# A two-layer recurrent block on eight cores: ScalarE's norms, the sums of LN1, y before V, and P's transpose put at other places in the order

## The reference

```python
# layer 0
xn = layernorm(x)
z = sigmoid(xn @ Wz.T + bz); h = xn @ Wh.T + bh
s = scan(h_t = (1 - z_t + 1e-8) * h_(t-1) + z_t * h_t)
g = silu((silu(xn @ wg.T / 127) * (xn @ wu.T / 127)) @ wd.T / 127)   # hidden 3072, int weights
x = x + s * g
# layer 1
xn = layernorm(x)
q, k, v = xn @ W_qkv.T
s = softmax(q @ k.T / 32) @ v                                      # one head of 1024, no mask
xr, xk = mix(xn, xn shifted by one token; mu_r), mix(...; mu_k)
g = silu(sigmoid(xr @ W_r) * (relu(xk @ W_k) ** 2 @ W_v))
x = x + s * g
```

## Time and profile before

| | us |
|---|---|
| median of 3 runs | 1410.72 |
| the runs | 1189.59, 1410.72, 1429.85 |
| the profiled execution | 1187.59 |
| its span on the slowest core (core 1) | 1186.4 |
| spans of the eight cores | 1180.2 to 1186.4 |
| PE busy | 1158.8 |
| DVE, ACT, POOL busy | 550.9, 259.5, 131.3 |

### The profile page before, as it was taken

How to read it: one execution, slowest core, us unless ns; L and a number is a source line. 1 busy time by engine, 2 the same in 40 slices (tenths; PEclk the granted TensorE clock), 3 DMA queues, 4 the chain that set the end, 5 groups by cost and what they waited for, 6 DMA issues and landing times.

```text
span 1186.4 us, 15396 instructions; the slowest of 8 cores (1180.2 to 1186.4 us)
## 1 busy us (share of the span) xinstructions
PE 1158.8 (98%) x5500; PEld 533.9 (45%) x5500; DVE 550.9 (46%) x707; ACT 259.5 (22%) x323; POOL 131.3 (11%) x241
## 2 busy tenths in 40 slices
PE   4999999999999999999999999999999999999988
PEld 3444444444444444444444444444444444444434
DVE  4244121456664765135566794011234445555545
ACT  3322211121223111112212733523110110111100
POOL 3121111101111111111011122220000000000000
PEclk9999999999999999999999999999999999999999
DMA  8795954455554684454552579994000105446664
GB/s 198 198 141 88 198 85 74 89 108 115 99 108 69 129 171 74 71 90 98 110 112 52 91 123 155 154 152 109 1 19 19 36 18 124 77 111 120 130 140 153
DMA packets 88074, 124.82 MB, mean 105 GB/s; under 512 B 39744, under 2 KB 44096, under 8 KB 88000
## 3 DMA queue, kind: packets, MB, share of 16 engines
q0 software_dynamic: 31104, 65.03, 34.9%
q1 hardware_dynamic: 56896, 58.81, 19.3%
HBM read 159.47 MB, written 20.97 MB: 152 GB/s over the span
## 4 chain that ended last, share of the span: by engine, by line
PE 96%; DMA 1%; DVE 1%; ACT 1%; issue 0%; POOL 0%; SPq 0%; DVEq 0%; ACTq 0%; POOLq 0%
PE PS L156 95%; PE PS L276 1%; DMA S<-S 1%; DMA S<-xtok 1%; ACT S L265 0%; DVE S L160 0%; DVE S L866 0%; ACT S L286 0%; SPq L127 0%; DVE BN L242 0%; PE PS L297 0%; DVE BN L243 0%; POOL MV L253 0%; POOL S L127 0%; PE PS L834 0%
## 5 line engine op out<-in xcount | busy, mean ns | idle before, releaser
L156 PE MATMUL PS<-S 128*128 128x512 bf16 x5264 | 1140.2, 379 | 6.8 <-DMA S<-S 3.9
L156 PEld LDWEIGHTS PS<-S 128*128 128x128 bf16 x5264 | 514.8, 98 | 622.4 <-issue 13.1
L160 DVE TENSOR_TENSOR S<-S,PS 128x512 bf16<-128x512 bf16 x96 | 66.0, 687 | 190.2 <-PE PS L156 180.8
L361 ACT ACTIVATE S<-PS 128x512 bf16<-128x512 f32 x96 | 57.3, 597 | 249.1 <-PE PS L156 234.0
L806 ACT ACTIVATE S<-PS,CB 128x2048 bf16<-128x2048 f32 x16 | 31.5, 1967 | 225.0 <-DVE CB L804 206.0
L160 DVE TENSOR_TENSOR S<-S 128x512 f32<-128x512 f32 (+2 forms) x60 | 62.9, 1048 | 8.6 <-ACT S L513 2.2
L802 DVE TENSOR_REDUCE CB<-PS 128x1 f32<-128x1024 f32 x32 | 39.2, 1224 | 55.7 <-PE PS L835 33.4
L703 DVE SCALAR_TENSOR_TENSOR S<-S,PS 128x1024 f32<-128x1024 f32 x16 | 19.5, 1221 | 82.1 <-PE PS L156 81.6
L424 ACT ACTIVATE S<-PS 128x512 bf16<-128x512 f32 x32 | 19.1, 597 | 173.2 <-PE PS L156 173.2
L127 POOL DMA_DIRECT2D S<-wg x48 | 27.9, 580 | 262.0 <-PE PS L156 234.0
L744 DVE CAST S<-PS 128x512 bf16<-128x512 f32 x32 | 22.1, 691 | 60.2 <-PE PS L156 60.2
(11 more groups left out here) (73 smaller groups left out, 417.6 us busy)
## 6 DMA issues: line engine op xcount, KB each, us to landing
S<-wg POOLq DMA_DIRECT2D x48, 256.0 KB, 5.1
S<-wu POOLq DMA_DIRECT2D x48, 256.0 KB, 5.8
S<-wd POOLq DMA_DIRECT2D x16, 768.0 KB, 7.8
S<-xtok SPq DMA_DIRECT2D x16, 512.0 KB, 10.1
S<-xt SPq DMA_DIRECT2D x16, 512.0 KB, 15.4
x1s<-S SPq DMA_DIRECT2D x16, 512.0 KB, 3.1
S<-x1s SPq DMA_DIRECT2D x32, 256.0 KB, 4.9
out<-S SPq DMA_DIRECT2D x31, 256.0 KB, 2.8
```

The costliest lines, as they stand in the source:

```text
L156: ins = te.matmul(dst, l, r, start=(i == 0), stop=(i == n - 1))
L160: return DVE.did(ve.tensor_mul(o, a, b))
L361: at = ACT.did(se.activation(sil, ps(bg), AF.Silu, scale=1.0 / 127.0))
```

## The change

In LN0, ACT's norm of the next tile is put ahead of its copy of the tile before, for tiles 1 and 2 and again for tile 6; the copy of tile 2 now stands behind DVE's norm of tile 3; the weight pairs are issued earlier on POOL; the warm matmuls go from 12, 12, 12 and 16 to 10, 10 and 12; transposes 4 and 5 are taken apart, 5 going to behind the second unit. In LN1, `sums` and `stat` become one step, so the list has one step less, and the place that took two steps to use them up takes one. The eight y units of the first quarter go ahead of the first eight V units. `p_transpose(j)` goes to directly behind `scores(j)`, except for the first tile of each quarter, where it stays behind the late units and now stands ahead of `recip`.

```diff
@@ -300,22 +300,30 @@
         ln0_rstd(0)
         POOL.after(xk_tok[1])
         w_pair()
-        for i in range(1, 4):
-            ln0_stats(i)
-            ln0_rstd(i)
-            ln0_norm(i - 1, True)
-            ln0_transpose(i - 1)
-            keep_warm(12)
+        ln0_stats(1)
+        ln0_rstd(1)
+        ln0_norm(0, True)
+        ln0_stats(2)
+        ln0_rstd(2)
         w_pair()
+        ln0_norm(1, True)
+        ln0_transpose(0)
+        keep_warm(10)
+        ln0_stats(3)
+        ln0_rstd(3)
+        w_pair()
+        ln0_norm(2, True)
+        ln0_transpose(1)
+        keep_warm(10)
         ln0_norm(3)
         ln0_stats(4)
         ln0_rstd(4)
         w_pair()
+        ln0_transpose(2)
         ln0_transpose(3, True)
-        keep_warm(16)
+        keep_warm(12)
         ln0_stats(5)
         ln0_rstd(5)
-        w_pair()
         ln0_norm(4, True)
         ln0_stats(6)
         ln0_rstd(6)
@@ -324,12 +332,12 @@
             ln0_norm(5, True)
             ln0_stats(7)
             ln0_rstd(7)
+            ln0_transpose(4)
             ln0_norm(6, True)
-            ln0_transpose(4)
-            ln0_transpose(5)
 
         def span1_b():
             ln0_norm(7)
+            ln0_transpose(5)
             ln0_transpose(6)
 
         early0 = [span1_a, span1_b, lambda: ln0_transpose(7, True), lambda: None]
@@ -525,7 +533,7 @@
                 DVE.after(t, st["rstd"][s], xn_ready)
                 xn1_tok[h, s] = mul(dst, tq, rb)
 
-            steps = [lambda: None, cast, sums, stat]
+            steps = [lambda: None, cast, lambda: (sums(), stat())]
             for s in range(2):
                 for q in range(2):
                     steps.append(lambda q=q, s=s: affine(q, s))
@@ -682,7 +690,7 @@
                 rk_free = ACT.did(se.activation(bf(KACT + o * 1024, 1024), rt, AF.Square))
                 w_done(wpos + o, mm)
                 if h == 0:
-                    step(late1, 2 if o == 7 else 1)
+                    step(late1)
                 else:
                     next(more, None)
             wpos += NC8
@@ -754,10 +762,10 @@
             bank_free[b] = y_tok[e, q]
 
         vq = collections.deque((tt, hf) for tt in range(NT) for hf in range(2))
+        for e in range(NC8):
+            y_unit(e, 0)
         for _ in range(8):
             v_unit(*vq.popleft())
-        for e in range(NC8):
-            y_unit(e, 0)
 
 
         ring = collections.deque([4, 5, 6, 7])
@@ -880,6 +888,8 @@
         for j in range(NT):
             q, i = j // 4, j % 4
             scores(j)
+            if i:
+                p_transpose(j)
             if j:
                 spread(j - 1)
             if q < 3:
@@ -891,8 +901,9 @@
                 late.extend([lambda q=q, d=2 * i: av_unit(q - 1, d), lambda q=q, d=2 * i + 1: av_unit(q - 1, d)])
             while len(late) > 2:
                 late.popleft()()
+            if not i:
+                p_transpose(j)
             recip(j)
-            p_transpose(j)
         while late:
             late.popleft()()
         bank_free[0:4] = s_free * 4
```

## The result

The changed kernel takes 1174.05 us (median of 4 runs, 1173.38 to 1176.33). Against the kernel before, the ratio is 0.9883, 95% interval [0.9862, 0.9903]: 1.2% less, some 14 us. The ratio leaves out executions in which the chip itself ran slower; the kernel before had two of these in its four runs (1410.72 and 1429.85 us, beside 1188.27 and 1189.59), which is why its median is no guide. The forecast, 1172.5 us in a range of 1167 to 1180, was 1.6 us too low. Where it was wrong is what it made of that time: 0.94 stood on "within 2%", taken as what a measurement cannot tell from no change, and the runs tell this change of 1.2% apart clearly.

A forecast was written before the change was run, and what follows sets the result against it. PE, busy 1158.8 of 1186.4 us, was taken as the bound, leaving 27.6 us of standing to win. Terms 7.6 + 1.9 + 0.05 + 5.6 = 15.1 off 1187.59 gave 1172.5 us, range 1167 to 1180 for 8 in 10.

The forecast's parts named there:

- within 2%: Whole kernel: time within about 2% of before, taken as what a measurement can't tell from no change; chance 0.94.
- The start: LN0 up to unit 3: ACT's new order removes PE's early waits; 7.6 us less, bounds 4 and 8.5.
- PE ahead of its loads: Gate and up units after LN0: PE, 8.1 us earlier, meets late weights; 0.5 us taken off.
- the late pair: Fifth weight pair, loaded beside x: its wu half lands at 52.7 us, stalling PE 0 to 0.9 us.
- The eighth pair: Eighth weight pair, behind the two big wd loads: between 0.7 us short and 3 to spare.
- LN1's step: LN1: DVE reads the sums at once, so PE's wait goes in full; 1.9 us less, bounds 0 and 1.9.
- y ahead of V: Before the first scores: a 1.0 us cast wait goes, about 0.95 for the fold's copy comes; 0.05 us less.
- P's transpose: Last attention quarter: PE's 3.9 us DMA wait and the 1.65 us clock fall behind it go; 5.6 us less.
- Rival A: LN0: the clock is not up when unit 0 begins; 1175.5 us, or 1177.5 with late weights; chance 0.18.
- Rival C: SP's queue: moved transposes make loads late, PE stands up to 4.6 us nine times; 1213 us; chance 0.04.
- Rival B: Last quarter: the last transpose, delayed by output traffic or queue, still ends PE's wait; 1176 or 1178 us; chance 0.08.

The follow-up runs named there:

- the split loads: The changed kernel with x tiles 12 to 15 loaded only once the weights of hidden tile 4 have landed: 1177.74 us, ratio 0.9909.

## Why the prediction was right, and where it was wrong

**The step that failed** is the one from the sum to the forecast: "About 2% is what a measurement of this kernel can tell from no change." From it I booked 1.3% less under "within 2%" with 0.94. No row that I had shows such a figure. In every kernel here the times behind a ratio lie within 0.3% of each other, and four runs give a ratio to 0.2%. A 1.2% gain with an interval that ends at 0.9903 is a gain. My own sum said as much: its terms were read from waits to 0.1 us, and no case with a chance above 0.04 in it ended at or above the time of before. The forecast should have been "faster, by about 1%, not by 2". The bounds were not added up rightly either: those of my four terms give 1171.1 to 1180.3 us, not the 1168 to 1177 that I wrote.

**The start** is the term that was mis-sized: priced at 7.6 us, it measured 5.7 alone (0.9952), and its 1.9 us are more than the 1.6 by which the whole forecast was too low. The mechanism was right: norm ahead of copy, the 2.28 us wait covered, the clock up. Three sizes were off. Unit 0 starts 7.7 us behind the first transpose, held by DVE's copy of tile 3, which ends 7.5 behind it; I had 7.5, set by the warm matmuls, with the copy done at 7.0. I said that the weight pair moved ahead on POOL changes nothing that PE waits for; it holds up the root of tile 3 and with it norm and copy, and the run with the pair behind it shows 0.4 us of that, masked by weights. The wait ahead of tile 6 is 0.7 to 1.1 us, not 0.5, because norm 5 waits 1.27 us for a bias that stands behind unit 0's product on DVE; the run with early biases shows it. Together, transpose 7 came 20.8 to 21.7 us behind the first and not 20.0, and unit 3 began at 34.3 on the slowest core, not 32.8. And the six of eight cores where the clock fell set the size: on the other two it is 4.4 to 5.3 us. The slowest core of before had the fall; the gain of the slowest core is smaller than that core's own, as another takes its place.

**PE ahead of its loads** was right in place and size: I took 0.5 off for a wait of 0 to 0.9 near 51.8 us; five cores of eight show none there, three 0.24 to 0.90, at 51.2 to 53.5. (A wait for a weight between 45 and 75 us was also on my list of signs of being wrong, against my own sum.) x was issued at 31.9, not 30.2, because the last of the first eight weight tiles, issued at 22.0, took 9.8 us to land. The reason that I gave for the late pair, less than an equal share beside x, is not what the trace shows. Between 47 and 49 us, when both are moving, weights (q0) and x (q1) have this of the DMA engines in the changed kernel (packets, MB, share of the 16 engines' time):

```profile
q1 hardware_dynamic: 71, 0.25, 48.8%
q0 software_dynamic: 82, 0.17, 47.8%
```

That is an equal share, as the Trainium skill has it, page DMA: Bandwidth & Descriptors, section "Queues, rings and completion order", by which each DMA engine takes turns between the queues packet by packet. I had taken from that rule that the pair would not be late; it was, with equal turns: 8.8 and 10.3 us with x, 4.9 and 5.5 without. On the three cores that wait, weights have 93, 81 and 100 packets in those 2 us beside 84, 81 and 72 of x. Part of it is the start: the first packet of the wg tile issued at 42.3 shows only behind 46 us, while x has some 90% of the engines, and in the kernel with the split loads, issued at 42.0, behind 44. Why it starts later beside x is open. The eighth pair, which I only noted, is what the split loads ran into.

**LN1's step**: 1.9 forecast, 1.9 measured (0.9984). **y ahead of V**: 0.05 forecast, not to be told from zero (1.0004), the exposed copy 0.9 us where I had 0.95.

**P's transpose**: 5.6 forecast, 5.5 measured (0.9954). That it fits so well is in part luck: I priced one core's 3.9 us and its fall of clock, while in that execution the wait was 1.9 to 4.5 us by core and only three cores had the fall. The landing was over-estimated: 4.8 us, where I had allowed 7.6 to 8.4; no output or load stands directly ahead of it on SP any more.

**Rival A** (clock not up) did not occur; without the warm matmuls it does, so the 32 that were kept are what kept it away. **Rival C** (slower by SP's queue) failed on both of its prices: SP is held 1.96 us, not 4.83, and moving one transpose or all twelve gives the same time (0.9955 and 0.9954). **Rival B** never came near.

## What to carry to other kernels

Where one engine is busy 98% of the span, the list of its waits, with the falls of clock behind them, is the whole budget: price each edit at its own wait, ask what is late next, and believe the sum; what counts as "no change" is the measured spread of that kernel, not a round figure. Putting one copy ahead of another only changes which is exposed; splitting the covering work so that some lies behind each covers both. A stage that is made faster runs into the loads behind it, so the queue of the loads has to be followed to the last place with little slack, not only to the first.

## What the runs showed of the hardware

A transposing DMA costs the issuing queue and its own landing more when plain DMAs have just been issued ahead of it. All sixteen of the kernel before, then of the changed one, where twelve are issued right behind exp, mostly into an empty queue (issue time in ns, then landing in us, both min/median/max):

```profile
L133 SPq DMA_TRANSPOSE S<-S x16: 1812/3932/5606, 883.7 to 1145.7; - x16
```
```profile
L133 SPq DMA_TRANSPOSE S<-S x16: 1817/1936/5368, 875.3 to 1131.2; - x16
...
DMA to landing us min/median/max: 4.3/4.4/8.7
```

The median of the issue falls from 3.9 to 1.9 us and that of the landing from 6.0 to 4.4. The run that moves only the last one shows the same for it: 1.97 us to issue and 4.6 to land, where that transpose in the kernel before takes 3.4 to 5.1 and 5.3 to 7.9 by core.

The clock's fall after a short wait is not fixed by the wait's length: in the kernel before 2.28 us ahead of transpose 5 brought it on core 1, and 2.60 us at the same place did not on core 5. Ahead of the fourth quarter, 2.03 us brought it on core 2 and 3.54 us did not on core 0.
